# Decay-scan sums of three layers moved from VectorE adds to accumulating transfers queued by GpSimd

## What is computed

```python
tf = sigmoid(sum(time_emb, -1))
decay = exp(-exp(w)) * (0.5 + 0.5 * tf)
ek = exp(min(k, 30)); ekv = ek * v
nf, df = scan(a * decay + ekv), scan(b * decay + ek)          # forward in time
nb, db = the same scans, backward in time
euk = exp(min(u + k, 30))
num = nf + nb - ekv + euk * v
den = df + db - ek + euk
out = sigmoid(r) * (num / max(den, 1e-8)) * (0.8 + 0.2 * tf)
```

## Time and profile before

| | |
|---|---|
| Three runs, median | 1021.62 us |
| Lowest, highest | 1020.59, 1023.24 us |
| Profiled execution, its own time | 1019.41 us |
| Its span in the profile | 1017.7 us |
| Busy: PE, DVE, ACT, POOL | 786.0, 592.2, 384.1, 236.5 us |
| Layer 0's pair loop on DVE | 119.9 to 180.2 us |
| Layer 1's block | about 182.5 to 346 us |

### The profile page before, as it was taken

How to read it: one execution, slowest core, us unless ns; L and a number is a source line. 1 busy time by engine, 2 the same in 40 slices (tenths; PEclk the granted TensorE clock), 3 DMA queues, 4 the chain that set the end, 5 groups by cost and what they waited for, 6 DMA issues and landing times. The chain is left out here.

```text
span 1017.7 us, 11188 instructions
## 1 busy us (share of the span) xinstructions
PE 786.0 (77%) x3629; PEld 588.3 (58%) x3629; DVE 592.2 (58%) x1268; ACT 384.1 (38%) x832; POOL 236.5 (23%) x216
## 2 busy tenths in 40 slices
PE   0776557656556625659999999999986999999995
PEld 0332435523233411448888788888876788888884
DVE  6889699369878377644655655555553333333333
ACT  2300512212122258645454454454453333343332
POOL 0401000140100347022012012012001255554543
PEclk9887778578988759869999999999996899999998
DMA  4000000731111500030010010100002231314321
GB/s 132 0 2 0 1 0 1 298 120 31 32 31 37 187 4 1 1 124 9 34 43 5 38 42 1 43 0 2 1 1 63 75 104 52 104 52 104 94 48 41
DMA packets 37374, 49.85 MB, mean 49 GB/s; under 512 B 18670, under 2 KB 30038, under 8 KB 35654
## 3 DMA queue, kind: packets, MB, share of 16 engines
q1 hardware_dynamic: 36262, 46.90, 14.8%
q0 software_dynamic: 768, 2.10, 0.6%
q10 hardware_dynamic: 288, 0.14, 0.1%
HBM read 43.00 MB, written 6.13 MB: 48 GB/s over the span
## 5 line engine op out<-in xcount | busy, mean ns | idle before, releaser
L2029 DVE TENSOR_TENSOR B_l<-bank,TW_l 128x512 f32<-128x512 f32 (+1 forms) x50 | 34.6, 692 | 140.8 <-PE bank L1974 140.8
L1648 ACT ACTIVATE EX<-EX,nm 128x128 f32<-128x128 f32 (+1 forms) x128 | 57.2, 448 | 108.5 <-DVE nm L1697 107.9
L1598 POOL TENSOR_TENSOR WL<-RAW,WH 128x512 fp32r<-128x512 f32 x32 | 41.1, 1290 | 231.6 <-ACT WH L1622 231.6
L2064 POOL TENSOR_TENSOR HL_l<-H_l,HH_l 128x512 fp32r<-128x512 f32 (+1 forms) x50 | 64.1, 1283 | 119.9 <-ACT HH_l L2043 119.9
L1974 PE MATMUL bank<-XH,WH_l 128*128 128x512 f32 (+1 forms) x200 | 79.8, 399 | 0.0
L1974 PE MATMUL bank<-XL,WH_l 128*128 128x512 f32 (+1 forms) x200 | 79.5, 398 | 0.0
L1974 PE MATMUL bank<-XH,WL_l 128*128 128x512 f32 (+1 forms) x200 | 79.5, 398 | 0.0
L134 POOL TENSOR_TENSOR WV<-EUK,V 128x512 f32<-128x512 f32 x16 | 23.5, 1475 | 178.4 <-DVE GAIN L219 178.4
L1711 DVE TENSOR_TENSOR AL<-bank,AH 128x256 fp32r<-128x256 f32 x64 | 27.1, 424 | 62.1 <-ACT AH L1663 62.1
L1751 PE MATMUL bank<-XH,WH 128*128 128x512 f32 x128 | 59.5, 465 | 3.9 <-DVE XL L1454 3.9
L2051 ACT ACTIVATE S_l<-bank 128x512 f32<-128x512 f32 (+1 forms) x50 | 30.1, 601 | 83.9 <-PE bank L1974 83.9
(11 more groups left out here) (307 smaller groups left out, 2089.9 us busy)
## 6 DMA issues: line engine op xcount, KB each, us to landing
RAW<-l_attn SPq DMA_DIRECT2D x8, 1024.0 KB, 5.0
WE<-l_experts SPq DMA_DIRECT2D x1, 6144.0 KB, 19.8
RAW_l<-l_experts SPq DMA_DIRECT2D x9, 512.0 KB, 3.9
TW_l<-routed SPq DMA_DIRECT2D x16, 256.0 KB, 5.2
RAW<-l_w SPq DMA_DIRECT2D x3, 1024.0 KB, 7.2
TW_l<-routed SPq DMA_DIRECT2D x14, 192.0 KB, 3.2
RAW_l<-l_experts SPq DMA_DIRECT2D x9, 256.0 KB, 4.7
sorted_x<-ZERO SPq DMA_DIRECT2D x1, 1920.0 KB, 24.4
```

Of the source, the lines that this page charges most:

```text
L1598: pool.tensor_tensor(WL[:, slot, c], RAW[:, slot, c], WH[:, slot, c].bitcast(F32), ALU.subtract).then_inc(w_low, 1)
L1648: act.activation(EX[:, s, a:b], EX[:, s, a:b], ACT.Exp, bias=nm[:, s, i:i + 1], scale=scale, accum_out=rs[:, s, i:i + 1]).then_inc(expd, 1)
L2029: v.tensor_tensor(self.B[0:rows, q % 2], self.k.banks[2 * (q % 2) + 1][0:rows], self.TW[0:rows, w % self.TWS, n * W:(n + 1) * W], ALU.mult ...
L2064: pool.tensor_tensor(self.HL[0:rows, q % 4], self.H[0:rows, q % 2], self.HH[0:rows, q % 4].bitcast(F32), ALU.subtract).then_inc(self.h_low, 1)
```

## The change

`add` is gone from DVE. A new function `gain_queue` has POOL queue the same four additions as transfers that add to their destination, in two pairs: `DF += DB` and `NF += NB` as soon as the chunk's 8 scans are done; then POOL waits until both have landed, and queues `DF += EUK` and `NF += WV`. `divide` waits for the second pair (`g_all`). The scan buffers are now used in turn by all chunks (`gain_slot` returns c % 2), and DVE's pieces are 3 per chunk in another order: `den` and `num` of chunk c, then `divide` of chunk c - 1. Layer 0's pair loop has one of its 12 pieces in each step. Layer 1 has 24 pieces, 4 in the steps of the shared expert and 20 over the 15 tiles. On POOL each chunk's `gain_queue` stands behind its `gain_pool`; in layer 1 chunks 8 and 9 are queued behind the 8 scatters.

```diff
 def gain_slot(c):
-    return c % 2 if gain_summed(c) else 0
+    return c % 2
 
+def gain_queue(pool, k, c):
+
+    layer, j = gain_layer(c)
+    slot = gain_slot(c)
+    n = c - gain_sum_no(c)
+    pool.wait_ge(k.g_scan, 8 * c + 8)
+    pool.dma_start(k.DF[slot][:], k.DB[slot][:], accum_op=ALU.add).then_inc(k.g_both, 16)
+    pool.dma_start(k.NF[slot][:], k.NB[slot][:], accum_op=ALU.add).then_inc(k.g_both, 16)
+    pool.wait_ge(k.g_both, 32 * n + 32)
+    pool.wait_ge(k.g_w, c + 1)
+    pool.dma_start(k.DF[slot][:], chunk(k.EUK[layer][:], j), accum_op=ALU.add).then_inc(k.g_all, 16)
+    pool.dma_start(k.NF[slot][:], k.WV[:, c % 2], accum_op=ALU.add).then_inc(k.g_all, 16)
...
-    def add(self):
...
     def divide(self, den=None, num=None):
...
-            v.wait_ge(k.g_add, 4 * (c - gain_sum_no(c)) + 4)
+            v.wait_ge(k.g_all, 32 * (c - gain_sum_no(c) + 1))
...
+def gain_pieces(first, last):
+
+    for c in range(first, last + 1):
+        if c < last:
+            yield c, "den"
+            yield c, "num"
+        if c > first:
+            yield c - 1, "divide"
...
             for c in range(2 * NCH):
                 gain_pool(pool, k, c)
+                if not gain_summed(c):
+                    gain_queue(pool, k, c)
...
-                if q < 4 * NCH - NPAIR:
-                    gain_piece(2 * q)
-                    gain_piece(2 * q + 1)
-                else:
-                    gain_piece(q + 4 * NCH - NPAIR)
+                gain_piece(v, k, *pieces[q])
...
-            for c in range(FIRST_GAIN1 + 2, LAYERS * NCH):
-                gain_pool(pool, k, c)
+            for c in range(FIRST_GAIN1, LAYERS * NCH):
+                if c >= FIRST_GAIN1 + 2:
+                    gain_pool(pool, k, c)
+                gain_queue(pool, k, c)
```

More of the change, by code:

```diff
@@ L86, in make_gain @@
     k.NF, k.NB, k.DF, k.DB = [[sb(f"{n}{i}", [P, W], F32) for i in range(2)] for n in ("NF", "NB", "DF", "DB")]
+    k.g_both = sem("g_both")
+    k.g_all = sem("g_all")
     k.expo = sem("expo")
@@ L165, in __init__ @@
         self.at = 2 * c
-    def piece(self, n):
-        (self.den_scans, self.num_scans, self.add, self.divide)[n]()
     def both_ways(self, of, fw, bw):
@@ L220, in divide, with gain_piece @@
                                ALU.min, ALU.mult).then_inc(k.g_done, 1)
+def gain_pieces(first, last):
[5 more added lines that the diff above has]
+            yield c - 1, "divide"
+def gain_piece(v, k, c, what):
+    g = GainVector(v, k, c)
+    if what == "den":
+        g.den_scans()
+    elif what == "num":
+        g.num_scans()
+    else:
+        g.divide()
 ORDER = [0, 2, 1, 3]
@@ L597, in low @@
                                 ALU.subtract).then_inc(hlo, 1)
-            def gain_piece(n):
-                GainVector(v, k, NCH + n // 4).piece(n % 4)
+            pieces = list(gain_pieces(NCH, 2 * NCH))
             for q in range(NPAIR):
@@ L719 @@
 FIRST_GAIN1 = 2 * NCH
[L722 to L729, removed]
+PIECES1 = list(gain_pieces(FIRST_GAIN1, LAYERS * NCH))
 STEPS1 = 4
@@ L961, in _ @@
             v.tensor_scalar(EID[:], which[:], float(E1 - 1), float(WCOLS1), ALU.min, ALU.mult).then_inc(pos, 1)
[L963 to L972, removed]
             for q in range(STEPS1):
@@ L977, in _ @@
                 v.tensor_tensor(HS[:, q], SS[:, q % 2], shared_banks[q % 2][1][:], ALU.mult).then_inc(s_h, 1)
-                piece(*PIECES1[q])
+                gain_piece(v, k, *PIECES1[q])
             for j in range(TILES1):
@@ L985, in _ @@
                 for c, what in pieces_after(j):
-                    piece(c, what)
+                    gain_piece(v, k, c, what)
         @block.tensor
```

## The result

| | before | after |
|---|---|---|
| Median of 4 runs each | 1021.80 us | 1044.30 us |
| Lowest, highest | 1020.59, 1023.24 us | 1033.17, 1047.41 us |
| Profiled execution, own time / span | 1019.41 / 1017.7 us | 1042.40 / 1040.7 us |
| Mean granted PE clock | 0.897 | 0.881 |

A forecast was written before the change was run, and what follows sets the result against it. DVE was taken to bound layer 0's pair loop, a ring of load, projections and store layer 1. Layer 0's -2.7 and layer 1's +4.1 us gave +1.4: 1023.0 us, no measurable change, range 1014 to 1037.

The forecast's parts named there:

- chain C: Time from a chunk's last scan to when its quotient may start: 2.53 us before, 10.6 us forecast with two pairs of transfers.
- the long chain's sign: C from 12 us on was to decide for the slower rival, which put C at 14.8 us.
- Short and long chain: Rivals on transfer latency. Short: C = 8.2, time 1013.9 us, chance 0.22. Long: C = 14.8, time 1040.5 us, chance 0.20.
- Layer 1, ring: Layer 1's tile loop of load, matmuls, store, next load: adding transfers delay loads by 0.33 us per chunk, +2.0 us.
- PE becomes layer 0's bound: Rival: gaps behind quotients lower PE's clock in layer 0's pair loop, so the 9.9 us aren't gained; total 1027, chance 0.08.
- Layer 0: Pair loop: additions removed -9.9, DVE waits for chunks 4 and 7 +6.5, moved `WV` +0.7; together -2.7 us.
- Layer 1, start: Up to the first tiles: faster scatter -1.3, transfers sharing DMA with first loads +0.7, later `HT` 1 +1.1 us.
- Layer 1, end: Behind the last tiles: the down projection's second half waits for the last quotient, done at 338.0 instead of 332.6; +1.6 us.

The follow-up runs named there:

- wv_early: The changed kernel with own buffers for the products of chunks 6 and 7, so POOL makes chunks 4 to 7's ahead of layer 0's loop: 1035.5 us.
- order_only: The changed kernel's new order and both scan buffers, but all sums as additions on DVE right ahead of each quotient, no adding transfers: 1025.3 us, ratio 1.0038.
- short_transfers: The changed kernel with each adding transfer cut to 16 of 512 columns, the other columns' sums left out: 1017.8 us, ratio 0.9977.
- layer1_only: Layer 1 as in the changed kernel, layer 0 as before with additions on DVE in the old order: 1037.9 us, ratio 1.0156.
- after_filled: The changed kernel with two extra matmuls, results unused, on PE in each of tiles 2 to 12 of layer 1: 1028.2 us, ratio 1.0089.
- before_filled: The kernel before with two extra matmuls per tile on PE in layer 1, results unused: 1013.4 us, ratio 0.9946.
- last_on_dve: The changed kernel, but chunks 7 and 15 summed by additions on DVE right ahead of their quotients: 1028.4 us, ratio 1.0109.
- layer0_only: Layer 0 as in the changed kernel, layer 1 as before with additions on DVE in the old order: 1021.7 us, ratio 0.9998.

## Why the prediction was wrong

**The chain C was right in layer 0.** 10.6 us were forecast and 10.3 measured there. At the end of layer 1 it was 12.5, over the 12 that the prediction had named as the long chain's sign. Short and long chain, which had 0.42 of the chance, both fall as they were written: where a quotient waited, C was neither near 8.2 nor near 14.8. The waits that I derived from the order were right as well: chunk 7 waited 3.95 us (forecast 4.2), chunk 4 2.40 in wv_early, once no stretched scan covered it (2.3), chunks 5 and 6 never. The Trainium skill's fit for a transfer queued by GpSimd (DMA: Bandwidth & Descriptors, section Anatomy of one DMA — SWDGE (gpsimd) path) gives an estimate of 2.6 us for 256 KB; these adding transfers took 3.4 and 4.3.

**The step that failed is "Layer 1, ring", +2.0 us: 18.0 were measured.** The prediction had itself named a period stretched by more than 1 us a tile as the sign that its mechanism is wrong, and it stretched by 1.8. I read the ring as waits and asked only how late a load would be. On that the estimate was not far off (3.3 us more waiting). I took the tile's matmuls as constant, and so put at nothing what the low clock adds to them, 15 us here, though the earlier trace rows say that PE idles 3 us in nearly every tile, and though the tiles of the kernel before already came in two kinds: 6.9 us apart, and 8.3 to 8.6. The earlier trace rows show two loads 8.61 us apart; I used that as the ring's period and did not ask why others are shorter. It was the low clock. Why the change sends more tiles there stays open: the order alone does not (order_only), the bytes are not needed (short_transfers), nor are late loads (layer1_only, wv_early). The rival "PE becomes layer 0's bound" was written, as its name says, for layer 0, where it didn't happen (0.94 from 120 to 150 us), and not for layer 1. The Trainium skill describes such a case (TensorE: Matmul & The Clock Gate, section HAM oscillation — how this bites in real kernels): short groups of matmuls between waits for DMA fall to the low clock again and again. after_filled and before_filled agree with it; that here only some tiles fall, 4 of 15 before and 11 after at the same wait of 3 us, stands beside it unexplained.

**"Layer 0", -2.7 us: -1.0 measured, with one term far off.** The terms as measured: -9.9 for the additions, +3.95 for chunk 7's wait, +6.1 for the stretched scans, -1.4 for the two stretched `HL` of the kernel before, which are gone. That gives -1.2. Chunk 4's wait, forecast at 2.3, was 0, since the first stretched scan covered it. I had put the third and fourth at +0.7 together, from a `WV` that met an `HL`; beside a scan and behind the issue of a transfer the same `WV` costs DVE 1.9 to 2.3 us. wv_early shows it by taking the products away. So the small miss of the sum hides two larger ones, of opposite sign.

**"Layer 1, start": the scatter's 1.3 us was not gained.** The 2.64 us scatter is gone, but beside scans six of the eight took 1.17 to 1.46 us, and all eight need 12.2 us from the first to the end of the last, 11.9 before. The sentence that the row speaks against the Trainium skill's rule (SBUF — State Buffer, section Who interferes with whom) claimed too much: one instance beside additions said nothing of the sum over eight. The same section holds that a DVE instruction with two SBUF inputs contends with a GpSimd instruction that reads SBUF; the stretched scans agree with it. The ring's start cost +2.3 us, +1.8 forecast.

**"Layer 1, end", +1.6 us: +4.7 measured.** The mechanism was the one forecast (PE stands in the middle of L1101 until the last quotient), but the chain took 12.5 us instead of 10.6 and the wait was 9.79 us instead of 6. last_on_dve takes 5 us off this end.

## What to carry to other kernels

Before relieving an engine, read the durations of the same instruction over time, not only the waits: where PE pauses in each round and the same matmuls have two durations, a change can lengthen instructions that it doesn't touch (here by 15 us in ten tiles). Spare matmuls in such a pause are cheap and worth trying first; here they alone gave 0.5 to 0.9%. In layer 0, moving sums from DVE to transfers shortened the loop where something else stands between the sum and its user (chunks 5 and 6), and cost their latency where nothing does (chunks 7 and 15). In layer 1, where DVE was busy but not waited for, it bought nothing in any kernel that computes its sums in full.

## What the runs showed of the hardware

- An adding transfer between SBUF tiles of 256 KB lands 3.3 to 3.4 us (median) after its issue when it is the first of a pair and 4.3 when it is the second. The first pair of a chunk takes 5.1 to 5.6 us in nine of twelve chunks, 3.2 when it carries a 32nd of the data. It took 6.3 us for chunk 8, beside the first loads of `XIN`, 6.9 for chunk 9, right behind chunk 8's second pair, and 7.3 for chunk 15, beside the last stores; that the neighbours cost this is likely and was not tested.
- POOL's tensor operation right behind the issue of a transfer held one DVE scan for 2.5 to 2.9 us instead of 0.66, three times out of three in the pair loop, and again in layer0_only and last_on_dve (2.58 to 2.98); without a transfer near it, 1.68. The issue alone held none.
- PE's granted clock from 231 to 266 us rose from 0.76 to 0.99 with the spare matmuls, while DMA was busier (0.54 to 0.62).
- What tips a tile to the low clock is open. At the first slow tile of the ring in the kernel after (projection at 240.20) PE had been idle 3.03 us, 2.98 before the fast one in the kernel before; 1.16 us for the second load and 0.76 for `HT` 1 had gone ahead. order_only had a later start still and only 4 slow tiles. No run isolates it.
